# A four-layer chain on one core: smaller first loads, and layer 0's sums closed by fours in the first three batches

## What is computed

```python
x = x + L0(x)   # x @ W.T + (x @ A[label]) @ Bw.T * 0.5      W: 1024x1024, A: 1024x32 by the batch's label
x = x + L1(x)   # elementwise: the group of |x| by 8 thresholds gives a delta and a zero point;
                # clip(round(x / delta) + zp, 0, 63), scaled back; 0 above the largest threshold
x = x + L2(x)   # x @ weight[adapter].T                      1024x1024, chosen by the batch's adapter
x = x + L3(x)   # (x @ B[adapter].T) @ A[adapter].T          rank 16
```

## Time and profile before

| | us |
|---|---|
| median of 3 runs | 488.97 (488.89 to 490.27) |
| the profiled execution's own time | 487.75 |
| its span in the trace | 486.0 |
| busy in the span: PE | 459.6 (95%) |
| DVE | 427.1 (88%) |
| ACT | 314.9 (65%) |
| DMA: mean rate over the span | 124 GB/s |

### The profile page before, as it was taken

One profiled execution on the slowest core, in us unless ns is written; L12 is line 12 of the kernel. 1 busy time (PEld: TensorE's weight loads), 2 busy tenths in 40 slices (PEclk: granted clock), 3 DMA queues, 4 the chain that ended last, 5 costly groups with the idle time before them and its releaser, 6 DMA issues.

```text
span 486.0 us, 7170 instructions
## 1 busy us (share of the span) xinstructions
PE 459.6 (95%) x2944; PEld 423.0 (87%) x2944; DVE 427.1 (88%) x387; ACT 314.9 (65%) x235; POOL 9.8 (2%) x16
## 2 busy tenths in 40 slices
PE   3997898999899999999999999999999999996995
PEld 3897898989898899989998899989998899884883
DVE  3689999999599997999699997999869997799963
ACT  5599969936396638966198544986259731966700
POOL 0002000000000000000000000000000000000000
PEclk9999899999999999999999999999999999998999
DMA  7883020074224642072423641044223442246022
GB/s 237 317 328 99 2 98 1 9 262 144 68 88 128 230 126 85 3 270 87 125 89 103 255 124 72 23 167 143 70 86 100 160 125 88 86 149 204 33 88 86
DMA packets 17172, 60.24 MB, mean 124 GB/s; under 512 B 2932, under 2 KB 4980, under 8 KB 13044
## 3 DMA queue, kind: packets, MB, share of 16 engines
q1 hardware_dynamic: 17140, 59.79, 35.7%
HBM read 51.39 MB, written 8.39 MB: 123 GB/s over the span
## 4 chain that ended last, share of the span: by engine, by line
PE 76%; DVE 11%; issue 5%; ACT 3%; DMA 2%; SPq 1%; DVEq 0%; ACTq 0%
PE l_ps L706 31%; PE l_ps L654 31%; PE l_ps L721 6%; PE bx_ps L738 3%; DVE quant L536 3%; DVE cand L510 2%; PE bx_ps L675 2%; PE l_ps L664 1%; PE l_ps L751 1%; DMA w_sb<-w 1%; DVE w_lo L457 1%; ACT cand L367 1%; DVE quant L530 1%; DMA adapter_ids<-adapters 1%; ACT x L337 1%
## 5 line engine op out<-in xcount | busy, mean ns | idle before, releaser
L706 PE MATMUL l_ps<-x,w_sb 128*128 128x256 f32 x896 | 195.6, 379 | 0.4 <-DVE x L497 0.4
L706 PEld LDWEIGHTS l_ps<-x,w_sb 128*128 128x128 f32 x896 | 169.2, 190 | 23.4 <-issue 0.8
L536 DVE COPY_PREDICATED quant<-mask,cand 128x2048 f32<-128x2048 int8 (+3 forms) x70 | 143.6, 2051 | 12.3 <-ACT mask L377 9.5
L377 ACT ACTIVATE mask<-magnitude,thr_bias 128x2048 fp8e5<-128x2048 f32 (+3 forms) x70 | 115.9, 1655 | 37.6 <-DVE quant L536 37.5
L367 ACT ACTIVATE cand<-x,inv_delta 128x2048 f32<-128x2048 f32 (+3 forms) x80 | 132.1, 1652 | 4.7 <-DVE quant L530 2.2
L510 DVE TENSOR_SCALAR cand<-cand,delta 128x2048 f32<-128x2048 f32 (+3 forms) x80 | 86.5, 1081 | 13.1 <-ACT cand L367 12.9
L654 PE MATMUL l_ps<-x_hi,w_hi 128*128 128x256 f32 x512 | 85.4, 290 | 9.6 <-DVE x_lo L463 8.2
L518 DVE TENSOR_SCALAR cand<-cand,lower,upper 128x2048 f32<-128x2048 f32 (+3 forms) x80 | 91.3, 1142 | 0.4
L654 PE MATMUL l_ps<-x_hi,w_lo 128*128 128x256 f32 x512 | 83.7, 286 | 1.1 <-DVE w_lo L457 1.1
L654 PE MATMUL l_ps<-x_lo,w_hi 128*128 128x256 f32 x512 | 83.8, 287 | 0.0
L654 PEld LDWEIGHTS l_ps<-x_hi,w_hi 128*128 128x128 f32 x512 | 72.1, 195 | 12.2 <-ACT w_hi L306 8.1
(11 more groups left out here) (48 smaller groups left out, 232.0 us busy)
## 6 DMA issues: line engine op xcount, KB each, us to landing
w_sb<-w SPq DMA_DIRECT2D x31, 1024.0 KB, 4.9
x_raw<-x SPq DMA_DIRECT2D x16, 512.0 KB, 5.6
out<-x SPq DMA_DIRECT2D x32, 256.0 KB, 2.2
w_sb<-w SPq DMA_DIRECT2D x8, 512.0 KB, 7.4
a_raw<-a SPq DMA_DIRECT2D x48, 64.0 KB, 4.5
a_raw<-a SPq DMA_DIRECT2D x8, 128.0 KB, 4.8
x<-w SPq DMA_DIRECT2D x1, 1024.0 KB, 5.9
a_raw<-b SPq DMA_DIRECT2D x4, 128.0 KB, 2.7
```

Of the source, the lines that this page charges most:

```text
L377: act.activation(mask[:, m % MASKS, 0:n], magnitude[:, 0:n], ACT.Relu, bias=thr_bias[:, k:k + 1], scale=STEEP, saturate=False).then_inc(ma ...
L536: dve.copy_predicated(y, mask[:, m % MASKS, 0:n].bitcast(I8), t).then_inc(merged, 1)
L706: last = nc.tensor.matmul(l2_bank(b, q)[:, i * S:(i + 1) * S], w2_tile(b, o)[:, k * P:(k + 1) * P], x2[:, b % SLOTS, k * S:(k + 1) * S], s ...
```

## The change

It has three parts.

1. **Loads.** x's first half and weight tile 0 come as two pieces each (512 columns, 256 KB), in the order x, w, x, w, each with a semaphore. ACT and DVE split them in the same pieces, and PE does tile 0 in three parts (k = 0 to 1, 2 to 3, 4 to 7). Weight tile 2 is issued ahead of the wait for the labels.
2. **The order at the start.** low_rank0(0) moves on PE from after the first tile to after the third; on ACT and DVE, low_rank_hi and low_rank_lo of batch 0 move to behind the split of the fourth weight tile. The split of weight tile 1 moves ahead of that of a0, that of tile 2 ahead of that of b0.
3. **Closing.** In batches 0 to 2, the first four tiles (o = 0, 2, 1, 3) are closed together after the fourth. Tiles 4 to 7 are closed one by one as before. Since two tiles share a bank and both sums are now open at once, only the even one's first matmul has the start flag. `AHEAD[0]` goes from 21 to 20: tile 20, the fifth of batch 2, moves from before the first layer 2 to behind it. low_rank3(0) stays after the third tile of that stage, so it now comes ahead of the last tile of batch 2, not behind it.

```diff
-AHEAD = (21, 28, 36, 43, 50, 57, 64, 64)
+AHEAD = (20, 28, 36, 43, 50, 57, 64, 64)
...
-            sp.dma_start(x_raw[:, 0:HW], x[0, :, 0:HW]).then_inc(x_loaded[0], 16)
-            load_w0(0)
+            sp.dma_start(x_raw[:, 0:CW], x[0, :, 0:CW]).then_inc(x_quarter_loaded, 16)
+            sp.dma_start(w0_stage(0)[:, 0:CW], w0[0, :, 0:CW]).then_inc(w0_half_loaded, 16)
+            sp.dma_start(x_raw[:, CW:HW], x[0, :, CW:HW]).then_inc(x_loaded[0], 16)
+            sp.dma_start(w0_stage(0)[:, CW:2 * CW], w0[0, :, CW:2 * CW]).then_inc(w0_loaded[0], 16)
...
             load_w0(1)
+            load_w0(2)
             sp.wait_ge(ids_loaded, 2 * 16)
             load_a0(0)
             for q in range(4):
                 sp.dma_start(a3_raw[q * QUAD:(q + 1) * QUAD, :], b0).then_inc(b0_loaded, 16)
-            load_w0(2)
...
+            def split_first_x(h):
+                cols = slice(h * CW, (h + 1) * CW)
+                act.wait_ge((x_quarter_loaded, x_loaded[0])[h], 16)
+                act.activation(x_hi[:, 0, cols], x_raw[:, cols], ACT.Copy).then_inc(x_hi_done, 1)
...
+            split_first_x(0)
             add_diag(0)
-            split_x(0, 0)
-            split_w0(0)
+            split_first_w0(0)
+            split_first_x(1)
+            split_first_w0(1)
             split_x(0, 1)
             add_diag(1)
+            split_w0(1)
             split_a0(0)
-            split_w0(1)
             add_diag(2)
+            split_w0(2)
...
-            low_rank_lo(0)
-            for n in range(2, T):
+            add_diag(3)
+            for n in range(3, T):
                 if n + 1 < T:
                     add_diag(n + 1)
+                if n == 4:
+                    low_rank_lo(0)
                 split_w0(n)
...
+                parts = ((0, 2), (2, 4), (4, 8)) if b == 0 and o == 0 else ((0, 4), (4, 8))
+                for first, end in parts:
+                    if b == 0 and o == 0:
+                        pe.wait_ge(w0_hi_done, 1 if first < HALF else 2)
+                        pe.wait_ge(x_split_done, (first + 2) // 2)
+                    elif b == 0:
+                        pe.wait_ge(w0_hi_done, w0_pieces(n))
+                    elif o == 0:
+                        pe.wait_ge(x_split_done, x_pieces(b, first // HALF))
...
-                                             start=(v is x_hi and w is w0_hi and k == 0), stop=False)
+                                             start=(o % 2 == 0 and v is x_hi and w is w0_hi and k == 0), stop=False)
...
                 main0(b, o)
-                if b > 2:
+                if b > 2 or i >= HALF:
                     close0(b, o)
-                elif i == 0:
+                elif i == (2 if b == 0 else 0):
                     low_rank0(b, 0)
-                elif i == 1:
-                    close0(b, ORDER[0])
-                    close0(b, o)
-                else:
-                    close0(b, o)
+                elif i == HALF - 1:
+                    for done in ORDER[:HALF]:
+                        close0(b, done)
```

More of the change, by code:

```diff
@@ L102, in build @@
         x_loaded = [sem(f"x_loaded{h}") for h in range(2)]
+        x_quarter_loaded = sem("x_quarter_loaded")
+        w0_half_loaded = sem("w0_half_loaded")
         a0_loaded = sem("a0_loaded")
@@ L179, in x0_halves, with x_pieces, w0_pieces @@
             return 2 * b + (first + n + HW - 1) // HW
+        def x_pieces(b, h):
+            return 2 * b + h + 2
+        def w0_pieces(n):
+            return n + 2
         block = ctx.enter_context(nc.Block())
@@ L428, in _ @@
             act.activation(table_warmup[:, :], ident[:, 0:1], ACT.Abs)
-            split_x(0, 0)
-            split_w0(0)
+            for h in range(2):
+                split_first_x(h)
+                split_first_w0(h)
             split_x(0, 1)
+            split_w0(1)
             split_a0(0)
-            split_w0(1)
+            split_w0(2)
             act.wait_ge(b0_loaded, 4 * 16)
             act.activation(b0_split[:, :], a3_raw[:, :], ACT.Copy, scale=0.5).then_inc(b0_hi_done, 1)
-            low_rank_hi(0)
-            for n in range(2, T):
+            for n in range(3, T):
+                if n == 4:
+                    low_rank_hi(0)
                 split_w0(n)
@@ L642, in main0 @@
                 dst = l0_ps[:, h, (o % HALF) * S:(o % HALF + 1) * S]
+                n = ORDER.index(o)
                 if o == h * HALF and b > 0:
                     pe.wait_ge(x0_done, 2 * (b - 1) + h + 1)
-                if b == 0:
-                    pe.wait_ge(w0_hi_done, ORDER.index(o) + 1)
-                for half in range(2):
-                    if o == 0:
-                        pe.wait_ge(x_split_done, 2 * b + half + 1)
+                parts = ((0, 2), (2, 4), (4, 8)) if b == 0 and o == 0 else ((0, 4), (4, 8))
[7 more added lines that the diff above has]
+                        pe.wait_ge(x_split_done, x_pieces(b, first // HALF))
                     for w, v in ((w0_hi, x_hi), (w0_hi, x_lo), (w0_lo, x_hi)):
-                        if b == 0 and w is w0_lo and half == 0:
-                            pe.wait_ge(w0_split_done, ORDER.index(o) + 1)
-                        for k in range(half * HALF, (half + 1) * HALF):
+                        if b == 0 and w is w0_lo:
+                            pe.wait_ge(w0_split_done, w0_pieces(n) if o > 0 or first == HALF else 1)
+                        for k in range(first, end):
                             nc.tensor.matmul(dst, w[:, o, k * P:(k + 1) * P], v[:, b % 2, k * S:(k + 1) * S],
-                                             start=(v is x_hi and w is w0_hi and k == 0), stop=False)
+                                             start=(o % 2 == 0 and v is x_hi and w is w0_hi and k == 0), stop=False)
             def close0(b, o):
@@ L663, in close0 @@
                         pe.wait_ge(b0_split_done, 1)
-                last = nc.tensor.matmul(dst, b0_split[:, o * P:(o + 1) * P], low_split[:, b % 2, :], start=False, stop=True)
+                last = nc.tensor.matmul(dst, b0_split[:, o * P:(o + 1) * P], low_split[:, b % 2, :], start=False,
+                                        stop=(o % 2 == 1))
                 if o in (HALF - 1, T - 1):
```

42 lines of the change are left out of this document (30 added, 12 removed).

## The result

| | median, us | lowest to highest | runs |
|---|---|---|---|
| before | 488.97 | 488.23 to 490.27 | 11 |
| changed | 486.60 | 484.52 to 487.42 | 11 |

The ratio is 0.9943 (95% interval 0.9929 to 0.9956), so the gain is between 2.2 and 3.5 us. The changed kernel's runs lie 2.9 us apart, those before 2.0.

What follows compares the result with a forecast made beforehand. DVE's chain to x2 was taken to bound the first layer 2; 55.03 + 3.0 + 1.7 − 1.4 = 58.3 us on, the second starts 4.0 earlier. Forecast 488.97 − 4.0 = 485.0 us (483.8 profiled), range 483.4 to 487.5.

Steps and rivals of the forecast that it cites:

- DVE's parameters come after 29: Start of DVE's chain: sign that the prediction is wrong; it expected them still at 27 to 28 us.
- PE's 2 us of waiting in front of layer 2: Before the first layer 2: PE would wait 2.2 us for x2; under 1 us would count as wrong.
- The wait of 1.7 inside layer 2: Third quarter of the first layer 2: PE would wait 1.7 us for DVE's addition on the first quarter's bank.
- batch 1's wait and its half-rate stretch: PE at batch 1's low_split: the 4.36 us wait and the 1.4 us lost at 1.2 GHz would go.
- The drain's 1.4: PE at tile 24, first of batch 3: the 1.40 us wait for ACT's drain would go.
- two rules weighed: Clock after idling: the trace's rows allowed a 1.4 us half-rate stretch after shorter waits; the skill made throttling the default, released by activity.
- Term (1) of that sum: Between the two layers 2: tile 20, moved behind the first layer 2, adds 3.0 us.
- low_rank0 ends at 20.7: Kernel start on PE: end of low_rank0 after three tiles, making DVE's chain only 0.15 us later.
- one or two more stretches at 1.2 GHz: Kernel start: rival with DVE's chain 1.4 to 2.8 us later, time 486.4 to 487.8; 20%, shared with late x data.
- The estimate of 1.8 us: Start loads: by the skill's batching rule, x's second half comes 1.8 us later, giving 486.8.
- All of PE's waits: Whole kernel: rival that every PE wait comes out as time, 9.1 us, giving 479.9; 3%.
- slower: Kernel start: rival with PE at 1.2 GHz throughout, DVE's chain 4.5 us later, plus 1.4, giving 490.9; 5%.

Runs made afterwards that it cites:

- fill: Changed kernel with batch 0's low_split before the seventh weight tile's split, AHEAD[0] = 21 and batch 2's four closes behind tile 20: 482.36 us, ratio 0.9864.
- ahead21: Changed kernel with AHEAD[0] = 21, tile 20 in front of the first layer 2 again: 483.49 us, ratio 0.9895.
- fill22: Changed kernel with batch 0's low_split late, batch 2's closes behind tile 20, AHEAD[0] = 22, stage 1's low_rank3 and layer3 one tile earlier: 480.25 us.
- whole_loads: Changed kernel with x's first half and weight tile 0 loaded in two issues, still split in pieces: 484.45 us, ratio 0.9915.
- late_low: Changed kernel with batch 0's low_split copy and subtraction moved from before the fifth weight tile's split to before the seventh's: 484.97 us, ratio 0.9916.
- after_again: The changed kernel measured again without any edit: median 485.69 us, ratio 0.9929; its profiled execution took 483.82 us.
- warm: Changed kernel with 18 float32 identity matmuls into an unused bank at PE's start, while it waits for data: 484.69 us, ratio 0.9914.
- start_only: Changed kernel with batches 1 and 2 closed as in the kernel before and AHEAD[0] = 21: 488.88 us, ratio 0.9999.

## Why the prediction was right, and by how much it was not

**Beside its own signs.** The prediction named as a sign of being wrong that DVE's parameters come after 29. In the first profile they do (the last of them at 29.59, the candidate behind it at 29.78), in the second they don't (27.52 and 27.72). PE's 2 us of waiting in front of layer 2 is there in both. The wait of 1.7 inside layer 2 is in neither, as a half-rate stretch took its place.

**The bound.** Right: once the closing waits go, DVE's chain to x2 sets the first layer 2, and not PE. Taking away PE's wait for low_split in front of x2 gave nothing (fill); putting work from later in front of it did (ahead21, fill22).

**PE's side.** Right: batch 1's wait and its half-rate stretch went, batch 2's is 1.26 us (0.7 expected), x2's 1.98 (2.2). The drain's 1.4 went as expected and comes back with tile 20 in front.

**From the first to the second layer 2.** 58.3 us expected; 58.48 in the first profile and 58.49 in the second, though its parts differ. With PE at full clock (whole_loads) the third quarter starts 15.45 us behind the first, as forecast (13.8 + 1.7 = 15.5), and the whole way is 58.44. With a half-rate stretch in the first quarters there is no such wait, and the three quarters take 22.64 in place of 20.72. What the stretch cost, 1.9 and not the 1.4 of the prediction, the wait gave back. A half-rate stretch was absorbed there, as forecast, but not two (late_low). Of the two rules weighed, the traces bear out the one that allowed for a stretch behind these shorter waits: it came in both profiles of the changed kernel.

```profile
81.06 14.05 PE L757 MATMUL l_ps<-x,w_sb 128*128 128x256 f32 x64 [1.98 <-DVE x L630]
96.51 7.14 PE L757 MATMUL l_ps<-x,w_sb 128*128 128x256 f32 x32 [1.40 <-DVE x L537]
```

**What was not asked.** Term (1) of that sum, +3.0 for tile 20, was taken as part of the change and not weighed against leaving the tile where it was. With it left there the way from the first candidate is 1.62 us shorter in both starts. The forecast was right for the change as made, but the change holds a loss that its own numbers (2.2 us of waiting in front of layer 2, a tile of 3.0) pointed to.

**The start of DVE's chain.** This is the term that was mis-sized: "low_rank0 ends at 20.7" and so +0.15 us. Of the 2.8 us by which the first profile misses the 483.8 forecast for a profiled execution, 1.9 are this term, 0.7 the tail and 0.2 the way between the two layers 2. It was right for after_again (20.7, ±0 us) and wrong for the first profile: 22.7, +2.06 us. I carried PE's pace over from a trace in which the first 24 matmuls run without a break; with pieces they run with gaps, and when the clock rises differs from execution to execution (the table under warm). The case stood among the rivals, as one or two more stretches at 1.2 GHz with 1.4 to 2.8 us, at 20%. It belonged into the forecast, since the order at the start puts DVE's chain behind it where before it was not.

**The tail.** Not thought of: a second stretch at 1.2 GHz between 443 and 450 us cost 0.7 us. PE waits 3.1 us there for DVE's addition, which stands behind batch 7's groups, so a small shift may change how long it stays down; that is argued, no run tested it. The profile from which the forecast was made has a tail of 20.15, and thirteen profiles lie from 19.50 to 21.46. That after_again met 483.8 so closely is therefore in part luck: its tail happened to be as short as that of the kernel before. The 1.2 us that the forecast adds between profile and median has the size of such a difference: start_only's profile, which is the kernel before but for its start and a tail of 21.35, took 488.97, the old median. What the runs without a trace had there isn't shown.

**The rivals.** "All of PE's waits" and "slower" were not seen. x's second half did come later than in the kernel before, by 0.8 us or more in the first profile (8.70 against at most 7.87) and 0.6 in the second (8.48); with the early pace low_rank0 ended at the forecast 20.7 all the same. The estimate of 1.8 us for it compared four pieces with one transfer of 1 MB, where the kernel before has two of 512 KB.

## What to carry to other kernels

When a change puts an instruction that waits for TensorE in front of a queue of ACT or DVE, price it with TensorE at its lower clock, not with the pace of the trace: early in a kernel the two can differ by 2 us from one execution to the next. Where an engine is about to become the second-latest, move work of the first into the gap in front of the meeting point, not out of it. And read two executions of one kernel before a difference of 2 us between two kernels is explained: split each time into stretches that the edit touches and stretches that it doesn't, and compare only the first.

## What was unexpected of the hardware

The same binary ran with PE's faster pace from before 12 us on in one execution (11 matmuls in the us from 12 to 13) and from about 16 us on in another (6 in that us, 12 from 14 to 16 against 19), with the same work in front of it, while the granted clock's column said 1.0 throughout. Idle times of 1.1 and then 1.98 us, with four closes between, in front of layer 2 were followed by half-rate stretches in late_low, two of 3.3 us in a row at 0.5 in the rows above, and by none in whole_loads, whose first two quarters took 14.05 us, two thirds of 20.72 and the last matmul's modelled end. Of the six profiles in which PE idles for 2.0 us in front of that layer 2, five have such a stretch behind it, warm among them, which has no idle time at its closes. Behind the 1.33 us of ahead21 and the 1.40 of the earlier trace rows there is none.
